# A fused adaptive FFN in float32: channel mixing in half-array matmuls, two batches at once

## What is computed

```python
h = gelu(embedding @ W0 + b0); h = gelu(h @ W1 + b1)
att = softmax(h @ W2 + b2)                                  # (64, 8)
agg_w = einsum('bk,koi->boi', att, weight)                  # (64, 64, 64)
agg_b = att @ bias_k
y = einsum('boi,bih->boh', agg_w, x) + agg_b[:, :, None]    # x is (64, 64, 1024)
bitlinear(x, w) = x @ (round(clip(w / (mean|w| + eps), -1, 1)) * mean|w|).T
out = x + bitlinear(bitlinear(y, w_gate) * bitlinear(y, w_up), w_down)   # 1024 -> 2752 -> 1024
```

## Time and profile before

| | |
|---|---|
| median of three runs | 1955.59 us |
| profiled execution: span | 1954.9 us (first to last instruction; about 0.7 below the median) |
| PE busy | 1897.3 us, 97% |
| PE weight loads busy | 897.0 us, 46% |
| DVE, ACT, POOL busy | 603.1, 440.8 and 131.6 us |
| channel mixing matmuls | 512 instructions, 69.0 us busy |

### The profile page before, as it was taken

The page is one execution under the profiler, slowest core; times in us unless marked ns, Lnnn a source line. Parts: engine busy times, 40 slices in busy tenths (PEclk is TensorE's granted clock), DMA queues, the critical chain, the costliest instruction groups (busy, mean ns, idle before and its releaser), DMA issues.

```text
span 1954.9 us, 22867 instructions
## 1 busy us (share of the span) xinstructions
PE 1897.3 (97%) x9127; PEld 897.0 (46%) x9127; DVE 603.1 (31%) x902; ACT 440.8 (23%) x712; POOL 131.6 (7%) x73
## 2 busy tenths in 40 slices
PE   5688999999999999999999999999999999999999
PEld 3344454445444454444544454444544445444444
DVE  6989941024310242103510144102431024200320
ACT  4766530212102120111202122021210212011100
POOL 0864400000000000000000000000000000000000
PEclk8899999999999999999999999999999999999999
DMA  7536210100001000010001000010000100000000
GB/s 283 197 121 237 86 55 32 44 1 1 22 23 43 1 1 27 17 44 1 6 32 50 0 1 17 28 44 1 1 22 23 44 0 1 27 17 1 1 11 33
DMA packets 27744, 77.91 MB, mean 40 GB/s; under 512 B 4160, under 2 KB 4480, under 8 KB 27648
## 3 DMA queue, kind: packets, MB, share of 16 engines
q1 hardware_dynamic: 27648, 76.43, 11.1%
HBM read 59.65 MB, written 16.78 MB: 39 GB/s over the span
## 4 chain that ended last, share of the span: by engine, by line
PE 92%; DVE 3%; issue 2%; ACT 2%; POOL 1%; DMA 0%; SPq 0%; DVEq 0%; ACTq 0%; POOLq 0%
PE ps L435 91%; DVE msk L913 1%; ACT g_r L665 1%; POOL ys L407 1%; DVE msk L905 0%; PE ps L517 0%; DVE aT L226 0%; ACT wgT L694 0%; DMA inter<-in_L_cond_b_dram 0%; POOL ab L418 0%; DVE wsum L784 0%; DVE ys L832 0%; ACT wuT L694 0%; POOL bbc L418 0%; DVE inter L953 0%
## 5 line engine op out<-in xcount | busy, mean ns | idle before, releaser
L435 PE MATMUL ps<-yp,wuT 128*128 128x512 f16 x2688 | 596.4, 380 | 0.0
L435 PE MATMUL ps<-wdT,inter 128*128 128x512 fp8e4 x2688 | 590.6, 379 | 0.0
L435 PE MATMUL ps<-yp,wgT 128*128 128x512 f16 x2688 | 586.6, 380 | 2.2 <-ACT wgT L694 1.1
L435 PEld LDWEIGHTS ps<-wdT,inter 128*128 128x128 f16 x2688 | 263.0, 98 | 316.2
L435 PEld LDWEIGHTS ps<-yp,wgT 128*128 128x128 fp8e4 x2688 | 262.1, 98 | 316.5 <-issue 5.1
L435 PEld LDWEIGHTS ps<-yp,wuT 128*128 128x128 fp8e4 x2688 | 262.3, 98 | 307.5 <-issue 8.3
L725 ACT COPY inter<-ps 128x512 f32<-128x512 f32 x168 | 98.5, 586 | 817.1 <-PE ps L435 817.1
L941 DVE SCALAR_TENSOR_TENSOR prod<-ps,inter 128x512 f32<-128x512 f32 x168 | 116.0, 690 | 328.3 <-PE ps L435 328.3
L739 ACT CAST inter<-prod 128x512 f16<-128x512 f32 x168 | 103.8, 618 | 441.2 <-DVE prod L941 441.2
L962 DVE SCALAR_TENSOR_TENSOR xr<-ps,osc,xr 128x512 f32<-128x512 f32 x64 | 48.0, 750 | 466.5 <-PE ps L435 466.5
L937 DVE SCALAR_TENSOR_TENSOR prod<-ps,g_r 64x512 f32<-64x512 f32 x8 | 5.6, 694 | 522.1 <-ACT g_r L733 522.0
(11 more groups left out here) (143 smaller groups left out, 646.4 us busy)
## 6 DMA issues: line engine op xcount, KB each, us to landing
xa<-in_x_dram SPq DMA_DIRECT2D x8, 2048.0 KB, 7.9
out_dram<-xr SPq DMA_DIRECT2D x64, 256.0 KB, 2.0
wdT<-in_L_ffn_w_up_dram SPq DMA_DIRECT2D x10, 512.0 KB, 4.8
ys<-in_L_ffn_w_down_dram SPq DMA_DIRECT2D x9, 512.0 KB, 4.2
xr<-in_L_ffn_w_down_dram SPq DMA_DIRECT2D x8, 512.0 KB, 4.5
inter<-in_L_ffn_w_gate_dram SPq DMA_DIRECT2D x7, 512.0 KB, 15.6
xr<-in_L_ffn_w_down_dram SPq DMA_DIRECT2D x8, 352.0 KB, 4.5
wdT<-in_L_ffn_w_gate_dram SPq DMA_DIRECT2D x5, 512.0 KB, 5.5
```

The lines of the kernel that those rows point to most:

```text
L435: return nc.tensor.matmul(o, l, r, start=start, stop=stop)
```

## The change

`conv` on PE now works at even k and does k and k + 1 together. Each matmul takes 64 rows: the channels of one batch of a pair, in the upper half (`h = 0`) or lower half (`h = 1`) of the array, with the 64 x 64 block of `ablk` as the moving operand. The upper half writes into `YB[0]`, the lower into `YB[1]`; in a bank stand the 2 blocks k times 4 pairs t times 64 columns. PE waits for the bias copy (`s_bbv`) already before k = 0, and for both banks to be emptied (`s_yv >= KH * c + k`) before each later pair. DVE adds each bank's 512 columns into `ys` in blocks of 64, at even k, two additions in a row; each counts 1 on `s_yv`. ACT's magnitudes wait for the pair's both additions.

```diff
--- before.py
+++ after.py
@@ -473,13 +473,18 @@
                 if k == 0:
                     pe.wait_ge(s_x, 16 * (c + 1))
                     pe.wait_ge(s_ablk, 2 * (c + 1))
-                if k == 1:
                     pe.wait_ge(s_bbv, c + 1)
-                if k >= 2:
-                    pe.wait_ge(s_yv, KH * c + k - 1)
-                for t in range(NT):
-                    last = mm(YB[k % 2][:, t * P:(t + 1) * P], xa[:, t, k * P:(k + 1) * P], ablk[:, t, :])
-                last.then_inc(s_y, 1)
+                if k % 2:
+                    return
+                if k:
+                    pe.wait_ge(s_yv, KH * c + k)
+                for j in range(2):
+                    for t in range(NT):
+                        at = (j * NT + t) * C
+                        for h in range(2):
+                            rows = slice(h * C, (h + 1) * C)
+                            last = mm(YB[h][:, at:at + C], xa[rows, t, (k + j) * P:(k + j + 1) * P], ablk[rows, t, rows])
+                    last.then_inc(s_y, 1)
 
             def norms(c):
 
@@ -626,7 +631,7 @@
         @block.scalar
         def _(act):
             def magnitudes(c, k):
-                act.wait_ge(s_yv, KH * c + k + 1)
+                act.wait_ge(s_yv, KH * c + k + 2 - k % 2)
                 if k >= 2:
                     act.wait_ge(s_l1, KH * c + k - 1)
                 elif not (isinstance(c, int) and c == 0):
@@ -823,13 +828,18 @@
 
             def conv(c, k):
 
-                dve.wait_ge(s_y, KH * c + k + 1)
+                if k % 2 == 0:
+                    dve.wait_ge(s_y, KH * c + k + 2)
                 if k == 0:
                     dve.wait_ge(s_bbv, c + 1)
                     if not (isinstance(c, int) and c == 0):
                         dve.wait_ge(s_yhi, KH * c)
                         dve.wait_ge(s_ylo, KH * c)
-                V.tensor_tensor(ys[:, k, :], YB[k % 2][:, :], bbc[:, :], ALU.add).then_inc(s_yv, 1)
+                for h in range(2 if k % 2 == 0 else 0):
+                    V.tensor_tensor(ys[:, k:k + 2, :].rearrange("p k (t h o) -> p k t h o", h=2, o=C)[:, :, :, h, :],
+                                    YB[h][:, :].rearrange("p (k t o) -> p k t o", k=2, o=C),
+                                    bbc[:, :].rearrange("p (t h o) -> p t h o", h=2, o=C)[:, :, h, :].unsqueeze(1)
+                                    .broadcast_to([P, 2, NT, C]), ALU.add).then_inc(s_yv, 1)
                 if k >= 1:
                     add_l1(c, k - 1)
                 if k == KH - 1:
```

## The result

The changed kernel takes 1980.17 us (median of 4 runs, 1977.58 to 1980.68) where the kernel before takes 1955.75 (4 runs, 1955.26 to 1957.69): a ratio of 1.0118, 95% interval 1.0104 to 1.0132 (formed over the executions, not from the two medians, whose quotient is 1.0125). It is slower by 24 us by the medians, by 23 by the ratio. The forecast was 1968.2 in a range from 1953 to 2021. The side was right, and the loads do run side by side as forecast, but the size was half of what came. In the experiments, one of 17 executions of the kernel before (2237 us) and one of 7 of the pairs on full rows (5197 us) stand apart and enter no ratio.

The account below looks back on a forecast made before the run. The prediction took TensorE (PE), busy for 97% of the span, as the bound. Steady loop 7.0, chunk 1 4.1 and chunk 0 1.5 made 12.6 us on 1954.9, so 1967.5, plus 0.7: 1968.2 us, range 1953 to 2021.

Parts of the forecast that it names:

- The side: Whole kernel: the change makes it slower, chance 0.50 + 0.30.
- the steady loop: Chunks 2 to 7: a pair of k takes 2.09 us instead of 1.80; 24 pairs, +7.0 us.
- The price of a k: Channel mixing on PE: one k costs 0.90 us, paced by 128-column float32 loads of about 0.108 us, whatever their rows.
- Loads side by side: Half-array weight loads on PE: one half's loads run beside the other's; chance 0.50, own range 1960 to 1976.
- the queued bound: Pair of k in the steady loop: if all 32 loads queue, 3.71 us, plus 1.91 a pair, +45.8 us.
- The change of row count: PE, around inserted matmuls: leaving and re-entering the 128-row form costs 0.31 us, 0.11 of it the first load.
- Chunk 1: Mixing in chunk 1: 12.3 us instead of 8.22, with three exposed waits of 1.5 us on DVE; +4.1 us.
- Chunk 0: Start-up mixing: DVE waits for two k at the start, four waits instead of three; +1.5 us (0 to 4).
- half clock at first: Chunk 0: PE at 1.2 GHz at first, 0.50 from 25 to 31 us.
- All loads queue: Rival for all mixing: loads of both halves follow one another; sum 63.3 us, 2019 us; chance 0.30.
- The halves gain: Rival for all mixing: halves work at once, each load pair costs half, a pair of k 1.21 us; 1943 us; chance 0.10.
- No change: Rival: the chip overlaps the row-count switch too, chunk 1's waits partly absorbed; within 4 us of 1955.6; chance 0.10.

Follow-up runs that it names:

- pairs on full rows: The change's pairs of k and waits, but with 128-row, 128-column matmuls as in the kernel before, in every chunk; 1962.59 us, ratio 1.0030.
- one half used twice: Chunks 0 and 1 as before; chunks 2 to 7 as changed, but both calls use the upper 64 rows; 2016.64 us, ratio 1.0308.
- halves in turn: Chunks 0 and 1 as before; chunks 2 to 7 as changed, but per k four upper-half matmuls, then four lower-half; 1975.92 us, ratio 1.0102.
- the steady loop alone: Chunks 0 and 1 as in the kernel before, chunks 2 to 7 as in the change; 1962.69 us, ratio 1.0036.

## Why the prediction was right, and where its size was off

The side and the steady loop were foreseen for the right reason. That the time fell into the range was in part luck: more than half of the loss comes from a term that the prediction does not have.

**The price of a k** (loading, not streaming) was right, and shown: half the columns cost 4.29 us a period for 4.35.

**Loads side by side**, my choice between the two bounds: right, two loads 5 to 7 ns apart every 0.111 us; the queued bound, had it been, was right as well (3.7 forecast, 3.8 measured with one half used twice). The reason I gave, that PE accepts a matmul whose weights still load, was only half of it: PE does draw the other half's load forward, but over some four couples, as the run with halves in turn shows.

**The change of row count**, 0.31 us from the bias matmul: right there (0.30 regained). A pair came to 0.24 more than two single k, where I had summed 0.29: the 32 loads take 16 rounds in all, and I had added 16 rounds to a first load that the 0.31 already holds. With the rounds at 0.111, 0.20 + 16 x 0.111 + 0.055 is the 2.03 to 2.04 that a pair takes. 7.0 us forecast, 5.8 by the periods, 6.3 by the run with the steady loop alone.

**Chunk 1**, +4.1 forecast, +9.0 measured, is the term that was mis-sized. The waits were right: three of 1.39 us on PE (I had 1.5). With 64 rows, 128 columns and the full clock the same four pairs took 12.3 us, from 257.07 to the first down matmul at 269.39, which is my 12.3; on full rows they took 12.1. What I left out is the clock. It fell from 2.4 to 1.2 GHz at the end of the second pair and came back 3.3 us into the down projection: two pairs 1.6 us longer each and some 1.7 us in the down matmuls, 4.9 in all, which with the 4.1 makes the 9.0.

**Chunk 0**, +1.5 forecast (0 to 4), +6.6 measured: outside its own bounds, for the same reason. I took the cold clock for the first pair only, and had the others at full as before. All four ran at 3.68 us, and what stood between them at the low clock too. The wait for the bias copy came to 0.9 us (25.96 to 26.86), where I had 0.5. At the clock of the kernel before, the waits would have cost about 2 us: chunk 1's mixing starts at 254.71 us before, at 256.59 with pairs on full rows and at 257.07 with 64 rows and 128 columns, 1.9 and 2.4 later.

So the step that failed is "half clock at first": the rows of before showed PE cold until 31 us, and I priced the edit as if the clock's course were given, when the runs show it to differ with the form of the edit. The rest of the sum, without the clock, is 5.8 + 4.1 + 2.4 = 12.3 us by these runs, where 12.6 was forecast; the clock, a term that the sum puts at nothing, makes 4.9 us in chunk 1 and 4.2 in chunk 0 (6.6 less 2.4).

**The rivals.** *All loads queue* (0.30) did not happen, though its price was real. *The halves gain* (0.10) is refuted: with the full-row load unchanged, halving the streaming gave 0.05 us a k, and two half-row loads every 0.111 us is what one full-row load took.

The Trainium skill states up to twice the speed for a dimension of 64 or less (TensorEngine Tiling, Theoretical Speedup). Nothing of it is reached in this case: its "up to" is bounded here by the 128 columns of float32 weights that each half still loads, 2.04 us for a pair against 1.80. The Trainium skill also states, in Key Properties on the same page, that different tiles can load weights in parallel; this case's trace agrees, with 5 to 7 ns between the loads of the two halves.

*No change* (0.10) fell with the 24 us.

## What to carry to other kernels

Before splitting a matmul to stream fewer columns, see which of the two sets the distance between starts: if the load does, and each part needs as many columns of weights, nothing is gained, and each excursion into another row count cost 0.24 to 0.30 us here. A small matmul with few rows inside a stream of full ones can be worth padding with zeros for the same reason: here it gave back 0.30 us each time. And price an edit near the start, or beside a wait, at both levels of TensorE's clock: the same 32 matmuls took 2.0 us within the dense steady loop and 3.68 among chunk 1's waits.

## What the hardware showed that was not expected

- The granted clock followed the form of the matmuls and the waits together, as in the table above: in chunk 1, with waits of 1.4 us, it stayed at 2.4 GHz for 128 columns and fell to 1.2 GHz for 64, at either row count (in pairs of 2.0 us, but of 3.7 us for 128 rows and 64 columns), and with 64 columns and no wait it stayed at 2.4 GHz for the 7.5 us that it was tried.
- It didn't rise, either: chunk 0's pairs in the change's form began at 1.2 GHz and the clock was still there after all four, at 50 us, though PE hardly paused; with 128 columns it was up by 31 us, before the second pair, and with 64 columns on all 128 rows at 44 us, in the third.
- With one half of the array used twice, 32 loads 0.11 us apart between two groups, the clock fell once in each steady chunk with PE always busy, where the change's own 24 pairs never lost it.
- PE draws a load of the other half forward over a few waiting matmuls: alternating calls gave 32 loads in 1.86 us, calls in blocks of four 32 in 2.47, one half alone 32 in 3.64.
